# Attention and routed experts on one core: the loop body written over 24 score units, and some products issued twice

## The chip, the cores and the metric

One Trainium2 chip, one of its cores. The metric is the device time of one execution in microseconds, lower is better. Engines are called PE (TensorE), DVE (VectorE), ACT (ScalarE), POOL (GpSimd) and SP (SyncE, which here only issues transfers).

## What is computed

A block with adaptive layer norms: differential attention, then a mixture of experts with the best 2 of 8. 32 sequences (batches) of 256 tokens, 128 channels, 16 heads with two query and key vectors of 8 channels each.

```python
mod = (silu(c) @ wmod).reshape(32, 6, 1, -1)
sa, ca, ga, sb, cb, gb = ...                # ga, gb kept away from zero
h = layernorm(x) * (1 + ca) + sa
Q, K, V = h @ W_q.T, h @ W_k.T, h @ W_v.T   # per head: Q1, Q2, K1, K2 of 8 channels, V of 16
attn = softmax(mask(Q1 K1) / sqrt(8)) - lam * softmax(mask(Q2 K2) / sqrt(8))   # causal
O = rmsnorm(attn @ V) * rms_scale * 0.2
x = x + ga * (O @ W_o.T)
h = layernorm(x) * (1 + cb) + sb
logits = h @ router_w.T + router_b          # top 2 of 8, gates by softmax
x = x + gb * sum over the two chosen experts of gate * (silu(h Wg) * (h Wu)) @ Wd
```

## The kernel before, in words

The program has two stages. The first is a loop over the batches that does the attention, the second layer norm, the routing, and scatters each token's row to its two experts' places in memory. The second stage takes the rows tile by tile through the experts, and a last part adds the results. The change touches only the loop.

The loop is written out in full, one `body(i)` for each engine and iteration, with semaphores between the engines. It is a software pipeline over batches. In iteration i the engines work on the load of i+3 (`bL`: statistics of the first norm), the projections of i+2 (`bA`), the row maxima of the scores of i+1 (`b1`) and its v (`bV`), the exponentials and outputs of i (`b2`), the last outputs and the normalisation of i-1 (`bC`), the output projection and residual of i-2 (`bW`), and norm, routing and scatter of i-3 (`bR`).

The backbone is 24 **score units** for each batch. Unit n is one PSUM bank of scores: four blocks of 128x128 where n % 6 is 0 or 1, two blocks of 128x256 otherwise. `scores(bm, be, n)` issues on PE the score products of batch i+1 (into `p_max`, two banks; lines 808, 811, with the mask products at 816), and interleaved with them the transposed score products of batch i (into `p_exp`, three banks; lines 837, 840). One kind sits in the upper half of the array's rows and the other in the lower half. DVE reduces the `p_max` bank to row maxima (`take_max`, line 1190). ACT takes the exponential of the `p_exp` bank (`exp_bank`, line 1009), and POOL masks it (`mask_bank`, line 1430). The maxima of half a batch (12 units) are split in two bfloat16 parts (`minus_max`, lines 1201 and 1204), turned by PE (`max_to_rows`, line 890), copied by ACT (`copy_max`, line 1014) and moved by SP into two rows of the query operand (`move_max`, line 771), so that the product of batch i subtracts them by itself.

Everything else is placed between the units. Before the change it is written over s = 0 to 15, where an even s has one unit and an odd s has two (n = s + s//2). On PE these are: `outputs(b, g)` (line 866) for each of 8 pairs of heads, at even s; the transposes of xn (909); the two projections (`project`, 882); the transposes of on_tok (918) and the output projection (930); the transposes of h2 (944); the router's product (950); the transposes of the outputs (`outputs_to_rows`, 876); v (957); and the ranks (966). They all write the two banks of `p_mix`; the order in which each bank is used is written by hand in MISC0 and MISC1, and `mix_free` lets a step wait for the reader of the step before it. Each engine takes its instructions strictly in the order in which they are written, so a step that waits holds up the units behind it.

One chain goes through memory. `project` (PE) -> `high_part` (ACT, line 1020) -> `rest_part` (DVE, 1210) -> `middle_part` (ACT, 1024) -> `low_part` (POOL, 1436) splits q (j = 0) and k (j = 1) of batch i+2 into three bfloat16 parts. When both low parts are there (`l_ready`), SP writes the parts to memory with nine transfers (lines 726 and 730), moves the maxima (771), and when the writes have landed reads them back in the layout that the score products want (`load_unit(b, 0)`, four transfers for each of two halves, lines 756 and 761), then `mods` (746) and the next `x` (707). The loaded operands are what unit 0 of the next iteration waits for:

```python
                if n in (0, NBANKS // 2):
                    wait(pe, unit_loaded[n // (NBANKS // 2)], b)
```

The reading in SP's body, which the change leaves as it is:

```python
                b = i.plus(2)
                if active(b):
                    wait(sp, parts_saved, b)
                    load_unit(b, 0)
```

## Time and profile before

| | |
|---|---|
| median of 3 runs | 1679.91 us (1677.23 to 1682.1) |
| the profiled execution's own time | 1678.91 us |
| its span, first to last instruction | 1677.1 us |
| mean granted TensorE clock | 0.903 of full |
| PE busy / PE weight loads busy | 1340.8 us (80%) / 940.4 us (56%) |
| DVE busy | 1228.7 us (73%) |
| ACT busy | 859.4 us (51%) |
| POOL busy | 857.3 us (51%) |
| DMA, mean | 90 GB/s |

How to read it: matmuls are pipelined, and the busy time of PE holds the depth of that pipeline, so 80% is not 80% of what PE could do. The granted clock is the share of full speed (2.4 GHz) that PE was given; 0.5 is 1.2 GHz. A busy share is a mean over two stages that have different limits. In the timelines, "x4" is four instructions of one kind merged into one line with the time from the first start to the last end, and the bracket is idle time of the engine before it, with what ended it.

### The profile page before, as it was taken

Reading aid. Unit: us, or ns where it says so; the run is one execution under the profiler, and the core shown is the slowest. Engines: PE = TensorE matmul, PEld = TensorE weight load, DVE = VectorE, ACT = ScalarE, POOL = GpSimd, SP = SyncE. Lnnn points to the kernel's source line nnn. Section 1 sums busy time; section 2 is a strip of 40 time slices with the busy share of each in tenths; the row PEclk is TensorE's granted clock in tenths of the full one; section 3 lists DMA queues with packets and bytes.
Section 4 is the critical chain, followed back from the end, with each engine's and each line's share of the span. In section 5 each row is a group of like instructions: output and inputs, shape, how many; then the busy total and the mean of one; then the engine's idle time right before and its main releaser. Section 6 shows DMA issues by size and latency. Waiting matters only on the chain. (4 is left out here: it accounts for less than half of the span.)

```text
span 1677.1 us, 44178 instructions
## 1 busy us (share of the span) xinstructions
PE 1340.8 (80%) x14048; PEld 940.4 (56%) x14049; DVE 1228.7 (73%) x3090; ACT 859.4 (51%) x1918; POOL 857.3 (51%) x1283
## 2 busy tenths in 40 slices
PE   1578888888888888888888888885199999999960
PEld 0345555555555555555555555553178888888850
DVE  3467887888888888888888888876756666666647
ACT  1156667666766676667666766664123333333320
POOL 0135566666666666666666666665323333333334
PEclk9999989998999899989998999896589999999985
DMA  5453444344434443444344434410111111111129
GB/s 203 99 111 76 112 109 101 86 111 109 105 85 108 112 105 84 111 111 105 83 111 111 106 83 108 105 39 17 43 44 44 44 44 46 43 44 45 44 76 296
DMA packets 182624, 151.73 MB, mean 90 GB/s; under 512 B 29555, under 2 KB 165369, under 8 KB 182068
## 3 DMA queue, kind: packets, MB, share of 16 engines
q1 hardware_dynamic: 165124, 122.11, 30.2%
q0 software_dynamic: 8448, 16.93, 3.3%
q10 hardware_dynamic: 8880, 10.49, 1.8%
q8 instruction: 97, 1.59, 0.4%
q14 instruction: 75, 0.61, 0.1%
HBM read 88.26 MB, written 60.51 MB: 89 GB/s over the span
## 5 line engine op out<-in xcount | busy, mean ns | idle before, releaser
L1190 DVE TENSOR_REDUCE mx<-p_max 128x2 f32<-128x512 f32 (+1 forms) x768 | 504.9, 685 | 198.3 <-PE p_max L816 188.9
L1009 ACT ACTIVATE probs<-p_exp 128x512 f32<-128x512 f32 x768 | 440.4, 601 | 239.7 <-PE p_exp L837 150.9
L1430 POOL TENSOR_SCALAR_AFFINE_SELECT probs<-probs 128x256 f32<-128x256 f32 (+1 forms) x768 | 366.3, 486 | 344.6 <-ACT probs L1009 333.3
L866 PE MATMUL p_out<-probs,v 128*32 128x256 f32 (+1 forms) x4096 | 253.3, 371 | 42.1 <-ACT ot L1000 35.7
L659 POOL DMA_INDIRECT pair_out<-on,v x136 | 133.7, 983 | 282.4 <-ACT on L569 274.6
L808 PE MATMUL p_max<-kt,qt 50*128 50x256 bf16 x1024 | 199.3, 293 | 35.6 <-ACT probs L1009 19.0
L866 PEld LDWEIGHTS p_out<-probs,v 128*32 128x32 f32 x4096 | 124.0, 119 | 145.2 <-POOL probs L1430 67.9
L837 PE MATMUL p_exp<-qt,kt 52*128 52x256 bf16 x1024 | 205.2, 289 | 0.0
L816 PE MATMUL p_max<-tri,ids 64*128 64x128 bf16 (+1 forms) x768 | 188.7, 253 | 0.0
L633 DVE TENSOR_TENSOR ot<-ot,p_max 128x512 f32<-128x512 f32 x136 | 93.5, 688 | 123.6 <-PE p_max L520 105.0
L816 PE MATMUL p_max<-tri,idb 64*128 64x128 bf16 (+1 forms) x768 | 172.3, 252 | 0.0
L1477 POOL DMA_INDIRECT rows_sorted<-h,idx x128 | 128.3, 1003 | 81.2 <-DVE idx L1392 53.0
L811 PE MATMUL p_max<-kt,qt 50*128 50x128 bf16 x1024 | 115.5, 235 | 60.2 <-DMA kt<-k_parts 27.7
L569 ACT ACTIVATE on<-p_exp,v 128x128 f32<-128x128 f32 x136 | 50.0, 368 | 195.8 <-PE p_exp L551 195.8
L551 PE MATMUL p_exp<-wd,rest 128*128 x1088 | 143.9, 275 | 0.9 <-ACT on L569 0.9
L551 PEld LDWEIGHTS p_exp<-wd,rest 128*128 128x128 f32 x1088 | 132.2, 192 | 1.3 <-issue 1.3
L811 PEld LDWEIGHTS p_max<-kt,qt 50*128 50x128 bf16 x1024 | 64.7, 100 | 118.7 <-issue 66.1
L563 ACT ACTIVATE ot<-p_exp 128x512 f32<-128x512 f32 x136 | 81.5, 599 | 93.3 <-PE p_exp L520 93.3
L808 PEld LDWEIGHTS p_max<-kt,qt 50*128 50x128 bf16 x1024 | 73.1, 99 | 93.5 <-DVE mx L1190 66.8
L840 PE MATMUL p_exp<-qt,kt 52*128 52x128 bf16 x1024 | 108.9, 232 | 0.2
L1000 ACT ACTIVATE ot<-p_out,out_scale 128x256 f32<-128x256 f32 x256 | 108.0, 483 | 0.0
L1436 POOL TENSOR_TENSOR part_l<-rest,part_m 128x512 bf16<-128x512 f32 x64 | 74.1, 1158 | 64.8 <-ACT part_m L1024 64.8
(174 smaller groups left out, 2750.5 us busy)
## 6 DMA issues: line engine op xcount, KB each, us to landing
qt<-q_parts SPq DMA_DIRECT2D x128, 192.0 KB
q_parts<-part_h SPq DMA_DIRECT2D x96, 128.0 KB, 1.9
kt<-k_parts SPq DMA_DIRECT2D x128, 96.0 KB
v<-rows_sorted SPq DMA_DIRECT2D x136, 65.0 KB, 1.8
q_parts<-part_m SPq DMA_DIRECT2D x64, 128.0 KB, 1.9
kt<-k_parts SPq DMA_DIRECT2D x128, 64.0 KB
qt<-pair_out SPq DMA_DIRECT2D x32, 256.0 KB, 5.0
mods<-mod_rows SPq DMA_DIRECT2D x32, 192.0 KB
```

The lines of the kernel that those rows point to most:

```text
L551: m = nc.tensor.matmul(p_down, hid_t[:, jd.c % 2, f * P:(f + 1) * P], wd[:, bass.ds(w0 + f * P, P)], start=(f == 0), stop=(f == FCH - 1))
L659: nc.gpsimd.indirect_dma_start(pair_out, bass.IndirectOffsetOnAxis(rows_in[:, j.slot, DIM:DIM + 1].bitcast(U32), 0), rows_out[:, j.slot, : ...
L808: yield nc.tensor.matmul(p_max[:, bank, j * SEQ:(j + 1) * SEQ], qt[rows, slot, h, P:SEQ], kt[rows, slot, h, :], start=(j == 0), stop=False)
L811: yield nc.tensor.matmul(p_max[:, bank, j * P:(j + 1) * P], qt[rows, slot, h, 0:P], kt[rows, slot, h, 0:P], start=(j == 0), stop=False)
L816: m = nc.tensor.matmul(blocks[:, :, c:c + LANE], (idb if half == t else ids)[masks, :], tri4[masks, 0:len(heads), :], start=False, stop=(h ...
L837: m = nc.tensor.matmul(p_exp[:, bank, j * SEQ:(j + 1) * SEQ], kt[rows, slot, h, 0:P], qt[rows, slot, h, :], start=True, stop=True)
L840: m = nc.tensor.matmul(p_exp[:, bank, j * P:(j + 1) * P], kt[rows, slot, h, P:SEQ], qt[rows, slot, h, P:SEQ], start=True, stop=True)
L866: m = nc.tensor.matmul(p_out[32 * j:32 * j + 32, pair, SEQ - n:SEQ], v[:, b.par, tile, 2 * g + head, :], src, start=(tile == 0), stop=(til ...
L1009: nc.scalar.activation(probs[:, quad % 2, k, :], p_exp[:, n % 3, :], ACT.Exp, scale=SCALE).then_inc(exp_done.sem, 1)
L1190: V.reduce_max(mx[:, w, tile, t, heads[0]:heads[-1] + 1], p_max[:, bank, :].rearrange("p (h k) -> p h k", h=len(heads)), AX.X, negate=True ...
L1430: G.affine_select(out=blocks, in_=blocks, compare_op=ALU.is_ge, fill=zero, base=0, pattern=[[0, count], [1, P]], channel_multiplier=-1).th ...
L1477: G.indirect_dma_start(rows_sorted, bass.IndirectOffsetOnAxis(idx[:, bR.par, k:k + 1].bitcast(U32), 0), h2[:, bR.par, k // NT, k % NT, :], ...
```

## The change

The four loop bodies of PE, ACT, DVE and POOL are written over u = 0 to 23, one score unit for each u, and the other steps are given a new u each. SP's body, the units themselves and the steps' instructions stay. The order of four uses of `p_mix` changes with them. And `scores` issues the exponentials' products of six units twice, both times to the same bank; only the second issue signals ACT.

```diff
-        MISC0 = [(ht_ready, 1, 2), (r_ready, 1, 2), (r_ready, 2, 2), (on2_ready, 4, -1),
+        MISC0 = [(ht_ready, 1, 2), (r_ready, 1, 2), (r_ready, 2, 2), (on2_ready, 3, -1),
                  (v_ready, 1, 1), (on2_ready, 1, 0)]
         MISC1 = [(nmt_ready, 2, 0), (ont_ready, 1, -2), (attn_scaled, 1, -2), (h2t_ready, 1, -3),
-                 (on2_ready, 3, -1), (route, 1, -3), (nmt_ready, 1, 1), (route, ROUTE_CARRY, -3),
+                 (route, 1, -3), (on2_ready, 4, -1), (nmt_ready, 1, 1), (route, ROUTE_CARRY, -3),
                  (on2_ready, 2, 0)]
...
-            def exp_unit(b, n):
+            def exp_unit(b, n, final=True):
...
-                    if j == len(heads) - 1:
+                    if final and j == len(heads) - 1:
                         m.then_inc(exp_ps.sem, 1)
                     yield m
 
+            DOUBLED = (12, 15, 16, 21, 22, 23)
+
             def scores(bm, be, n):
 
+                if n in DOUBLED and active(bm):
+                    for _ in exp_unit(be, n, final=False):
+                        pass
                 for _ in itertools.zip_longest(max_unit(bm, n), exp_unit(be, n)):
                     pass
...
-                for s in range(NH):
-                    n = s + s // 2
-                    scores(b1, b2, n)
-                    if s % 2:
-                        scores(b1, b2, n + 1)
...
+                for u in range(NBANKS):
+                    scores(b1, b2, u)
+                    if u in (0, 2) and active(bC):
+                        outputs(bC, PAIRS - 2 + u // 2)
+                    if u in (6, 8, 12, 14, 18, 20) and active(b2):
+                        outputs(b2, 2 * (u // 6 - 1) + u % 6 // 2)
...
-                    if s in (4, 6) and active(bA):
-                        low_part(bA, (s - 4) // 2)
...
+                    if u in (8, 12) and active(bA):
+                        low_part(bA, (u - 8) // 4)
```

Where each step stands, before (by the unit after which it is issued) and after:

| engine | step | after unit, before | after unit, now |
|---|---|---|---|
| PE | outputs, pairs 6 and 7 of i-1 | 0, 3 | 0, 2 |
| PE | outputs, pairs 0 to 5 of i | 6, 9, 12, 15, 18, 21 | 6, 8, 12, 14, 18, 20 |
| PE | transposes of xn | 0 | 3 |
| PE | max_to_rows, second half of i | 2 | 1 |
| PE | project q, project k | 2, 5 | 4, 7 |
| PE | transposes of on_tok; output projection | 3; 5 | 3; 5 |
| PE | transposes of h2; router | 6; 11 | 7; 9 |
| PE | outputs_to_rows of i-1, both tiles | 8, 9 | 10, 11 |
| PE | v; max_to_rows of i+1; ranks | 12; 14; 15 | 13; 14; 16 |
| PE | outputs_to_rows of i, both tiles | 20, 21 | 17, 19 |
| ACT | xn; h2's norm | 23; 23 (iteration before) | 0; 1 |
| ACT | copy_max of i; ht | 2; 0 | 1; 3 |
| ACT | copies of outputs | 5, 11, 17, 23 | 3, 9, 15, 21 |
| ACT | ont | 3 | 4 |
| ACT | high_part; middle_part of q | 2; 5 | 5; 7 |
| ACT | high_part; middle_part of k | 5; 8 | 8; 11 |
| ACT | h2t; copy of h2; gates | 6; 9; 15 | 7; 12; 13 |
| ACT | v; copy_max of i+1; logarithm; root | 12; 14; 18; 20 | 14; 15; 19; 20 |
| DVE | minus_max of i; on_tok | 0; 0 | 0; 1 |
| DVE | statistics of i+3 | 7, 9 | 2, 3 |
| DVE | rest_part q, k; xtmp | 3, 6; 6 | 6, 9; 7 |
| DVE | normalise of i-1; of i | 9, 10; 21, 22 | 11, 13; 19, 21 |
| DVE | logits; top 8; index, choice | 12; 13; 13 | 10; 11; 14, 15 |
| DVE | minus_max of i+1; statistics of i-2 | 12; 12, 13 | 12; 15, 16 |
| DVE | sum of squares; roots; rows | 16; 16, 21; 18 | 17; 18, 22, 23; 20 |
| POOL | h2 times, h2 plus | 0, 3 | 2, 4 |
| POOL | low_part q, k | 6, 9 | 8, 12 |
| POOL | residual; sum; squares | 8; 12; 14 | 9; 14; 15 |
| POOL | four scatters | 18, 20, 21, 23 | 21, 22, 22, 23 |

On DVE the steps of an odd s stand between its two units, on the other engines behind both.

## Rows read from the trace of the kernel before

**Rows 1.** The page's 40 slices of the span, PE's busy tenths and the granted clock:

```profile
PE   1578888888888888888888888885199999999960
...
PEclk9999989998999899989998999896589999999985
```

**Rows 2.** Timeline of PE (start us, us, line, out<-in), the first and the last start of unit 0:

```profile
60.41 0.60 PE L811 MATMUL p_max<-kt,qt 50*128 50x128 bf16 x4 [16.44 <-DMA kt<-k_parts]
...
1092.04 0.21 PE L811 MATMUL p_max<-kt,qt 50*128 50x128 bf16 x1 [1.14 <-issue]
```

**Rows 3.** Windows of half an iteration (stretch, its length, busy us of each engine, PEclk, DMA):

```profile
core 0: us, PE busy (x) PEld busy (x) DVE busy (x) ACT busy (x) POOL busy (x), PEclk, DMA share, GB/s
603.72:620.99 17.27, 12.85 (x169) 7.84 (x170) 15.82 (x49) 9.50 (x24) 10.59 (x17) 0.90 0.52 143
620.99:636.69 15.70, 14.60 (x190) 9.73 (x190) 12.05 (x27) 12.95 (x30) 11.13 (x20) 1.00 0.29 62
636.69:654.40 17.71, 14.13 (x170) 8.46 (x170) 15.58 (x49) 9.65 (x24) 10.78 (x18) 0.81 0.57 140
```

**Rows 4.** Windows before and inside two low stretches of the clock:

```profile
610.14:613.55 3.41, 1.86 (x26) 1.12 (x26) 3.28 (x10) 1.89 (x5) 0.99 (x3) 1.00 0.40 91
...
613.55:616.97 3.42, 3.25 (x34) 1.96 (x35) 2.72 (x13) 1.54 (x5) 1.23 (x2) 0.50 0.65 151
...
644.27:651.10 6.83, 6.56 (x62) 3.81 (x63) 5.37 (x18) 3.85 (x9) 2.99 (x5) 0.50 0.80 165
```

**Rows 5.** Timeline of SP's queue (start us, us of issuing, line, out<-in, how many):

```profile
603.55 1.43 SPq L726 DMA_DIRECT2D q_parts<-part_h  x3
...
608.42 2.41 SPq L771 DMA_DIRECT2D qt<-nmt  x4
...
614.10 1.14 SPq L761 DMA_DIRECT2D kt<-k_parts  x3
...
636.51 1.43 SPq L726 DMA_DIRECT2D q_parts<-part_h  x3
```

**Rows 6.** Timeline of POOL around low_part(1):

```profile
601.99 0.41 POOL L1430 TENSOR_SCALAR_AFFINE_SELECT probs<-probs 128x256 f32<-128x256 f32 x1
...
602.36 1.16 POOL L1436 TENSOR_TENSOR part_l<-rest,part_m 128x512 bf16<-128x512 f32 x1
...
605.24 0.64 POOL L1430 TENSOR_SCALAR_AFFINE_SELECT probs<-probs 128x512 f32<-128x512 f32 x1 [0.81 <-ACT probs L1009]
```

**Rows 7.** Windows after the loads were issued:

```profile
618.00:618.50 0.50, 0.50 (x16) 0.26 (x8) 0.50 (x2) 0.35 (x1) 0.41 (x2) 1.00 0.86 279
618.50:619.00 0.50, 0.50 (x9) 0.42 (x4) 0.47 (x3) 0.00 (x0) 0.43 (x1) 1.00 0.35 115
```

**Rows 8.** The page's DMA issues (KB each, median us from issue to landing):

```profile
q_parts<-part_h SPq DMA_DIRECT2D x96, 128.0 KB, 1.9
```

**Rows 9.** Timeline of PE, the steps of the first half:

```profile
624.39 1.10 PE L882 MATMUL p_mix<-ht,wqk 128*128 128x256 f32 x4 [0.30 <-ACT ht L1037]
...
631.73 0.44 PE L944 MATMUL p_mix<-idf,h 128*128 128x128 f32 x2 [0.33 <-DVE xtmp L1308]
...
633.50 0.28 PE L808 MATMUL p_max<-kt,qt 50*128 50x256 bf16 x1
...
633.62 0.27 PE L808 MATMUL p_max<-kt,qt 50*128 50x256 bf16 x1
...
633.93 0.86 PE L866 MATMUL p_out<-probs,v 128*32 128x256 f32 x16
...
634.72 0.66 PE L876 MATMUL p_mix<-idf,ot 128*128 128x128 f32 x4
```

**Rows 10.** Timeline of DVE in unit 6:

```profile
631.26 0.41 DVE L1308 TENSOR_TENSOR xtmp<-p_mix,mods 128x256 f32<-128x256 f32 x1
631.59 0.68 DVE L1210 TENSOR_TENSOR rest<-p_mix,part_h 128x512 f32<-128x512 f32 x1
```

**Rows 11.** Timeline of ACT, copies of the outputs and h2's activations:

```profile
620.94 0.84 ACT L1000 ACTIVATE ot<-p_out,out_scale 128x256 f32<-128x256 f32 x2
...
622.42 0.88 ACT L1104 ACTIVATE h<-xres,neg_mr,rstd 128x128 f32<-128x128 f32 x2
```

More of the change, by code:

```diff
@@ L921, in body @@
                         m.then_inc(ont_ps.sem, 1)
-                    if s == 1 and active(bA):
+                    if u == 3 and active(bA):
+                        mix_free(pe, i, 0, 0)
+                        wait(pe, xn_ready, bA)
+                        for tile in range(NT):
+                            m = nc.tensor.transpose(p_mix[:, 0, tile * P:(tile + 1) * P], xn[:, tile, :], idf[:])
+                        m.then_inc(xt_ps.sem, 1)
+                    if u == 4 and active(bA):
                         wait(pe, ht_ready, bA)
                         project(i, bA, 0, 1)
-                    if s == 3 and active(bW):
+                    if u == 5 and active(bW):
                         mix_free(pe, i, 1, 2)
@@ L952, in body @@
                         m.then_inc(lg_ps.sem, 1)
-                    if s == 8 and active(bV):
+                    if u == 10 and active(bC):
+                        outputs_to_rows(i, bC, 1, 0, 0, 3)
+                    if u == 11 and active(bC):
+                        outputs_to_rows(i, bC, 1, 1, 1, 5)
+                    if u == 13 and active(bV):
                         mix_free(pe, i, 0, 4)
@@ L1095, in body @@
-                    if s == 15 and active(bW):
-                        if not (bW.static and bW.c < 2):
-                            wait_half(act, scattered[bW.par], bW.plus(-2))
-                        wait(act, h2t_ps, bW.plus(-2))
-                        wait(act, h2_copied, bW.plus(-2))
-                        settle(act)
-                        for tile in range(NT):
-                            c = NT * NH + NT + tile
-                            nc.scalar.activation(h2[:, bW.par, 0, tile, 0:DIM], xres[:, bass.ds(bW.n * SEQ + tile * DIM, DIM)],
-                                                 ACT.Identity, bias=neg_mr[:, NT + tile:NT + tile + 1],
-                                                 scale=rstd[:, c:c + 1]).then_inc(xn2_ready.sem, 1)
@@ L1300, in body @@
                                         ALU.mult).then_inc(on_ready.sem, 1)
-                    if s == 2 and active(bA):
+                    if u == 2 and active(bL):
+                        wait_half(dve, x_loaded[bL.par], bL)
+                        settle(dve)
+                        statistics(bL, 0, stats1)
+                    if u == 3 and active(bL):
+                        for tile in range(NT):
+                            mean_and_variance(bL, 0, stats1, tile)
+                    if u == 6 and active(bA):
                         rest_part(bA, 0)
-                    if s == 4 and active(bW):
+                    if u == 7 and active(bW):
                         wait(dve, wo_ps, bW)
@@ L1339, in body @@
-                    if s == 9:
-                        if active(bR):
-                            wait(dve, route, bR, 1)
-                            settle(dve)
-                            for tile in range(NT):
-                                V.max(top8[:, tile, :], lg[:, tile, :]).then_inc(route.sem, 1)
-                        if active(bW):
-                            for tile in range(NT):
-                                mean_and_variance(bW, 1, stats2, tile)
+                                normalise(bC, 1, 0, 0, k)
@@ new lines, in body @@
+                            if active(bR):
+                                if k == 0:
+                                    wait(dve, route, bR, 1)
+                                    settle(dve)
+                                V.max(top8[:, k, :], lg[:, k, :]).then_inc(route.sem, 1)
+                    if u == 12 and active(b1):
+                        minus_max(b1, 0, 0)
+                        minus_max(b1, 0, 1)
+                    if u == 13 and active(bC):
+                        for k in range(2):
+                            normalise(bC, 1, 1, 1, k)
@@ L1393, in body @@
-                    if s == 14:
-                        if active(b2):
-                            for k in range(2):
-                                normalise(b2, 0, 0, 0, k)
-                        inverse_roots(i, [1, 2, 3, 4])
-                    if s == 15 and active(b2):
+                        wait(dve, route, bR, 10)
+                        V.reciprocal(hrow[:, 0:NT, DIM + 1], gden[:]).then_inc(route.sem, 1)
+                        V.tensor_scalar(hrow[:, :, DIM].bitcast(I32), hrow[:, :, DIM].bitcast(I32), float(2 * SEQ), None, ALU.add)
@@ L1469, in body @@
                         G.tensor_tensor(osq[:], o[:], o[:], ALU.mult).then_inc(osq_ready.sem, 1)
-                    if s in (12, 13, 14, 15) and active(bR):
-                        k = s - 12
+                    for k in {21: (0,), 22: (1, 2), 23: (3,)}.get(u, ()):
+                        if not active(bR):
+                            continue
                         if k == 0:
```

230 lines of the change are left out of this document (108 added, 122 removed).

## The prediction, before the changed kernel was built

> **What bounds the kernel now.** I read the page's 40 slices first. TensorE (PE) is 0.8 or more busy in nearly every slice of the attention loop and all but full in the expert stage behind it; the granted clock dips again and again in the loop, and behind it only where PE has little to do [rows 1]. The change touches only the loop, so the rest of the time (from about 1,210 us to the end) is taken as it is. The first products of score unit 0 run at 60.41 us in the first iteration that has them and at 1092.04 us in the last [rows 2]: 31 iterations in 1031.6 us, 33.28 us each. All that follows is an estimate of that period.
>
> Next I cut one iteration at unit 0 and unit 12 [rows 3]. The first half (620.99 to 636.69) takes 15.70 us, at full clock; PE is busy 14.60 us of it, VectorE (DVE) only 12.05. The second half takes 17.27 or 17.71 us; there DVE is busy 15.82 or 15.58 us and PE 12.85 or 14.13. So there are two regimes: PE sets the pace in units 0 to 11, DVE in units 12 to 23. In the second half the granted clock falls: PE is busy 1.86 us of the 3.41 us before the fall and 3.25 of 3.42 after it, at half clock [rows 4]. Yet where the low stretch is twice as long (6.83 us at 0.50, [rows 4]), the half is only 17.71 - 17.27 = 0.44 us longer. DVE hides most of the loss.
>
> Third, the queue that no busy share shows. SP saves the parts of q and k of the batch two ahead to memory, then loads them back into the layout of the score products. Unit 0 of the next iteration waits for that load. In one round the saves start at 603.55, as low_part(1) ends on POOL (602.36 + 1.16 = 603.52) [rows 5, 6]. Nine saves, four moves of the maxima (608.42 to 610.83) and eight loads follow, and the last loads are issued until 615.24 [rows 5]. Then come mods and x; the DMA engines are still 0.86 busy at 618.0 to 618.5 and 0.35 in the next half microsecond [rows 7]. From an issue to its landing a save takes 1.9 us [rows 8]. So the last load lands between 615.24 + 1.9 = 617.1 and 619.0. The round trip from the end of low_part(1) to the landed load is thus 13.6 to 15.5 us. I take 15.0: eight large loads share the engines, so the end of their traffic is nearer than the landing of one transfer. Unit 0 comes at 620.99, 17.5 us after low_part(1). The slack is about 2.5 us, today.
>
> **The change, part by part.** *Low part.* low_part(1) moves from after unit 9 to after unit 12 on POOL; SP's order is untouched. Before: unit 9 starts at 633.50, the saves at 636.51, 3.0 us later [rows 9, 5]. After: unit 12 has four blocks to mask, 0.64 us instead of 0.41 [rows 6], so 3.2 us after the start of unit 12. The half from unit 0 to unit 12 takes 15.7 us now. The trip then begins at 15.7 + 3.2 = 18.9 us after unit 0 instead of 636.51 - 620.99 = 15.5, even if nothing else gets slower. With 15.0 us for the trip the period is 33.9 us or more.
>
> *Steps of the first half.* Their work on PE is the same, but what covered their waits moves. (a) The transposes of h2 wait for xtmp on DVE, 0.33 us now, with one pair's output products (0.79 us, 633.93 to 634.72 for the next pair) in between [rows 9]. After, both are in unit 7 with nothing between, and DVE still has to reduce unit 7 first, then xtmp (0.33 us to the next start, [rows 10]): 0.8 us more. (b) The first projection waits 0.30 us for ht [rows 9]. After, ACT does h2's two activations (0.88 us) and the copies of the outputs (0.84 us, [rows 11]) in units 1 and 3, ahead of ht; PE has one score unit and little more to do meanwhile: 0.6 us more. (c) outputs_to_rows in unit 10 must wait for rest_part(1) in unit 9 (0.68 us, [rows 10]), where three units lay between them: 0.5 us more. Together 1.9 us; the bounds are nothing (the engines' queues absorb them) and 3.5 us (max_to_rows in unit 1, now one step behind minus_max, added, and each wait a whole reduction longer). So unit 12 starts 17.6 us after unit 0, the trip starts at 20.8 and lands at 35.8.
>
> *Doubled products.* In units 12, 15, 16, 21, 22 and 23 each exponential's product is issued twice. One of 256 columns takes the array 0.12 us (633.50 to 633.62, [rows 9]), so 0.24 us a unit, 1.4 us an iteration. They run in the other half of the rows beside the products of the maxima, and lie in the half where DVE leads: I cost them at nothing, with 1.4 us as the bound if DVE's lead is gone.
>
> *Second half.* Spreading the DVE steps moves no work out of it (one normalise comes in at unit 13, the logits and top-8 go out). Its floor stays near 15.8 us of DVE, so it could end at 17.6 + 15.8 = 33.4. The load at 35.8 is 2.4 us later: unit 0 waits, and PE, which is in order, holds the outputs and transposes of that unit back with it.
>
> *The clock.* Today it falls after the thinnest 3.41 us of PE work, and it comes back while PE is nearly always busy [rows 4]. A PE that stands before unit 0 is a new thin place, just ahead of the half in which PE leads. If the low stretch reaches 5 us into it, PE's 5 us at full clock become up to 7.5; but ACT and DVE set part of that pace. Between 0 and 2.5 us, I take 0.8, nearer to the 0.44 us that a longer low stretch costs now.
>
> Sum: 17.6 + 3.2 + 15.0 + 0.8 = 36.6 us a period, 3.3 over 33.28. Over 31 periods that is 103 us. The first three have fewer stages and so an earlier trip: less 2 us each, 97 us. The profiled execution took 1678.91 us (span 1677.1), 1.0 us under the median of 1679.91: forecast 1678.9 + 97 = 1776 us.
>
> **Rivals.** *The clock holds.* The fall follows the thinnest stretch of PE work [rows 4]; the doubled products and the even spread fill it, and PE runs at full clock throughout. The second half then runs at DVE's pace, 15.8 us for 17.5 on average [rows 3], and with a first half as now (15.7) the period is 31.5, 1.8 less: 31 x 1.8 = 56 us, 1623 us. With half of the added waits left it is 32.4 and 1652. For it: the low stretches lie just where the doubled units are. Against it: the loads must have landed by unit 0, so the trip must start 31.5 - 15.0 = 16.5 us after unit 0, and 18.9 is the earliest that I find. It decides only if the trip takes under 12.6 us, below my 13.6. Chance 0.10. (The Trainium skill says the same of the clock in "TensorE: Matmul & The Clock Gate", Part 1: the default state is throttled, and activity releases it. By that rule alone this rival would be the likeliest, at 1623 us; the trace agrees that the clock follows PE's activity, but the rule knows nothing of the transfer.)
>
> *The transfer stays hidden, the waits stay.* The trip takes 13.6 us, or the waits of the first half are absorbed: 33.4 to 33.6 us, +0.3 a period, 1688 us; with the low stretch kept (17.6 + 17.5 = 35.1) 1735. For it: what waits ahead of a projection today waits only 0.3 us. Against it: 17.6 + 3.2 + 13.6 = 34.4 is still over 33.4. Chance 0.18, two thirds of it slower than 1684.
>
> *The change does not do what it says*: the doubled products land in the same idle time and the clock falls as before. That changes the forecast by less than 1 us a period, and is inside its range.
>
> **The numbers.** Forecast, the transfer bound: chance 0.72, its own range 1698 (33.9 us a period, no added waits) to 1832 (38.2: 3 us of added waits, 15.5 for the trip, 0.8 to 1.3 for the clock). A measurement of this kernel tells about 0.3%, 5 us, from no change. Faster 0.10; within 0.3% 0.06, from the second rival; slower 0.84. The range of 1690 to 1832 leaves the first rival and the far tail out.
>
> **What would show it.** Right: a PE wait of 2 to 3 us for the DMA of kt before unit 0 in every iteration, the first save some 21 us after unit 0, the trip still near 15 us, a period near 36.6, and a thin DVE and PE just before unit 0. The steps: waits of about 1 us before the transposes of h2 and before the first projection, 0.5 before those of outputs_to_rows in unit 10. Wrong: unit 0 released by DVE's reduction of unit 22, as now. If then the granted clock is 1.00 through the loop the first rival holds; if the first half is 15.7 us, my added waits were absorbed; if loads land in 12 us, I misread the trip.

## The result and the profile after

| | before | after |
|---|---|---|
| median of 4 runs, us | 1681.01 (1677.23 to 1684.34) | 1845.24 (1839.65 to 1849.4) |
| profiled execution, us (span) | 1678.91 (1677.1) | 1849.4 (1847.6) |
| period, first to last start of unit 0 | 33.28 | 38.51 |
| low clock per iteration, us (mean of iterations 6 to 26) | 6.3 | 11.4 |
| load landed ahead of unit 0, us (mean of the same) | 2.9 | 0.05 |

The ratio of the medians on one chip is 1.0976 [1.0937, 1.1014]: 9.8% slower. The forecast was 1776 us and the range ended at 1832. The sign and the mechanism came as forecast, the size did not. The loop's 31 periods, from 60.85 to 1254.79 us, take 1193.9 us for 1031.6 before ([rows 2]): 162 of the 170 us between the two spans.

The page's slices and the row of unit 0's products, against [rows 1]:

```profile
PE   1577787888887888888887788877619999999970
...
PEclk9988889888878898888887978899658999999995
...
L811 PE MATMUL p_max<-kt,qt 50*128 50x128 bf16 x1024 | 118.7, 246 | 104.6 <-DMA kt<-k_parts 102.2
```

PE's row, which had 8 nearly everywhere, now has many 7s; the clock's, which mostly stood at 9 with dips, stands at 8. PE waited 102.2 us in all for the DMA of kt (27.7 before; some 16.5 of each lie ahead of the first iteration). PE's longest waits in the stretch from 300 to 1100 us (engine, line and what it waited for; us in total, times, longest):

```profile
PE p_max L811 <- DMA kt<-k_parts: 45.5, 20, 3.6
PE p_mix L966 <- DVE both L1358: 43.1, 21, 2.1
...
PE p_mix L938 <- DVE xtmp L1312: 22.3, 20, 1.1
...
PE p_mix L881 <- DVE rest L1208: 8.5, 21, 0.4
...
PE p_mix L887 <- ACT ht L1061: 4.2, 9, 0.6
```

The first row is the forecast wait for the load, 2.3 us a time (0.8 to 3.6). The third, fourth and fifth are the three added waits (a), (c) and (b): 1.1 us for xtmp, 0.4 for rest_part in unit 10, up to 0.6 for ht in nine of the 21 iterations. The second was not forecast: in unit 16 the products that rank the experts wait 2.05 us for DVE's sum `both`. Before, the same wait was 23.6 us over 21 times in 300 to 1000 us, 1.1 us each.

Windows of two iterations of after, unit 0 to unit 12 and unit 12 to unit 0 (columns as in [rows 3]):

```profile
core 0: us, PE busy (x) PEld busy (x) DVE busy (x) ACT busy (x) POOL busy (x), PEclk, DMA share, GB/s
593.50:614.48 20.98, 19.46 (x191) 12.18 (x192) 11.36 (x23) 13.06 (x28) 11.05 (x19) 0.76 0.24 49
614.48:633.96 19.48, 13.40 (x184) 8.38 (x184) 16.70 (x52) 10.30 (x24) 11.35 (x18) 0.91 0.57 125
...
672.18:690.79 18.61, 15.24 (x191) 10.10 (x192) 12.19 (x27) 12.87 (x29) 12.52 (x21) 1.00 0.26 60
690.79:709.74 18.95, 13.39 (x185) 8.40 (x184) 16.54 (x52) 10.30 (x24) 11.06 (x17) 0.90 0.57 131
```

The two first halves hold the same 191 products. At full clock they keep PE busy for 15.24 us, at a mean of 0.76 for 19.46; the half grows from 18.61 to 20.98 us. Over iterations 6 to 26, the six first halves with no low clock take 18.4 us on average, the six with 6.8 us of it 19.8, the six with 10 us 21.0 and the three with 13 us 22.3. Before, the low stretches lay in the second half and the first ran at 1.00 ([rows 3]). Where the clock falls shows in windows around the two waits:

```profile
619.00:622.20 3.20, 1.10 (x18) 0.87 (x19) 3.16 (x12) 1.95 (x5) 2.86 (x5) 1.00 0.82 246
622.20:626.70 4.50, 4.50 (x52) 2.71 (x53) 3.66 (x13) 1.87 (x4) 1.22 (x3) 0.70 0.25 68
630.50:633.96 3.46, 0.04 (x1) 0.00 (x1) 2.05 (x7) 1.05 (x3) 2.65 (x4) 1.00 1.06 164
633.96:640.70 6.74, 6.74 (x67) 3.46 (x68) 4.71 (x9) 3.99 (x9) 4.42 (x7) 0.52 0.69 148
640.70:646.00 5.30, 4.99 (x56) 3.62 (x54) 2.51 (x6) 4.08 (x9) 1.87 (x4) 0.97 0.01 2
```

Ahead of the ranks PE is busy 1.10 of 3.20 us, and the clock falls behind it. Ahead of unit 0 it is busy 0.04 of 3.46 us, waiting for kt, and the 6.74 us that follow run at 0.52, which is the lower level (1.2 GHz) for nearly all of it. Then it is back. Means over iterations 6 to 26: 4.5 us low behind the first wait (units 17 to 20), and 6.7 us in the first half, behind the second wait. That one does not come every time: six first halves have none of it, behind waits for kt of 0.8 to 1.5 us, and fifteen have 6.8 to 13.2 us, behind waits of 1.2 to 3.6 us. Units 0 to 5 take 11.1 us on average, for 8.7 where the clock holds (e6, below).

The transfer, on SP's queue:

```profile
617.66 1.43 SPq L726 DMA_DIRECT2D q_parts<-part_h  x3
...
622.53 3.25 SPq L771 DMA_DIRECT2D qt<-nmt  x4
...
627.97 1.14 SPq L761 DMA_DIRECT2D kt<-k_parts  x3
...
630.47 0.33 SPq L756 DMA_DIRECT2D qt<-q_parts  x1
```

and on POOL and PE, the two ends of the round trip:

```profile
616.48 1.15 POOL L1435 TENSOR_TENSOR part_l<-rest,part_m 128x512 bf16<-128x512 f32 x1
```

```profile
633.96 0.23 PE L811 MATMUL p_max<-kt,qt 50*128 50x128 bf16 x1 [3.42 <-DMA kt<-k_parts]
```

low_part(1) ends at 617.63, 3.15 us behind unit 12 (614.48), the first save starts at 617.66, and the eight loads that unit 0 needs are issued until 629.11. Their data land 4.8 us later, and unit 0 starts at 633.96, 16.3 us after low_part(1). (The row at 630.47 already belongs to the loads for unit 12, which the queue issues until 633.53.) Means over iterations 6 to 26: 11.3 us from the end of low_part(1) until the last load for unit 0 is issued and 4.3 us from there to the landing, 15.6 us together. Before, these were 11.5 and 3.75 us, 15.25 together. So a period is 20.1 + 3.2 + 15.6 = 38.9 us, where the forecast sum had 18.4 + 3.2 + 15.0 = 36.6.

### The profile page after: what moved, and what is told of

It reads as the page before. It is cut to its first block, busy times and chain, and to the rows that moved or that the text cites. A ratio compares the mean times of both kernels' runs of the same rounds, so it can differ in the third digit from the quotient of the medians.

```text
span 1847.6 us, 45079 instructions
## 1 busy us (share of the span) xinstructions
PE 1444.4 (78%) x14482; PEld 1004.4 (54%) x14483; DVE 1231.5 (67%) x3090; ACT 881.8 (48%) x1918; POOL 862.3 (47%) x1283
## 4 chain that ended last, share of the span: by engine, by line
PE 54%; SPq 16%; DMA 9%; issue 8%; DVE 6%; POOL 4%; ACT 3%; POOLq 0%; DVEq 0%; ACTq 0%
PE p_out L871 8%; PE p_exp L551 6%; DMA kt<-k_parts 6%; PE p_exp L520 6%; PE p_max L520 5%; PE p_max L808 5%; PE p_mix L887 4%; SPq L726 4%; SPq L771 4%; PE p_max L816 4%; PE p_mix L544 3%; PE p_mix L881 3%; PE p_max L811 3%; SPq L761 2%; PE p_mix L930 2%
## 5 line engine op out<-in xcount | busy, mean ns | idle before, releaser
L1188 DVE TENSOR_REDUCE mx<-p_max 128x2 f32<-128x512 f32 (+1 forms) x768 | 526.1, 686 | 361.9 <-PE p_max L816 357.9
L1009 ACT ACTIVATE probs<-p_exp 128x512 f32<-128x512 f32 x768 | 454.3, 598 | 477.2 <-PE p_exp L837 245.5
L1429 POOL TENSOR_SCALAR_AFFINE_SELECT probs<-probs 128x256 f32<-128x256 f32 (+1 forms) x768 | 373.6, 489 | 538.6 <-ACT probs L1009 535.5
L871 PE MATMUL p_out<-probs,v 128*32 128x256 f32 (+1 forms) x4096 | 266.9, 388 | 14.4 <-POOL probs L1429 13.3
L837 PE MATMUL p_exp<-qt,kt 52*128 52x256 bf16 x1334 | 234.8, 291 | 0.2 <-ACT probs L1009 0.2
L808 PE MATMUL p_max<-kt,qt 50*128 50x256 bf16 x1024 | 219.6, 300 | 12.4 <-DVE mx L1188 12.4
L816 PE MATMUL p_max<-tri,idb 64*128 64x128 bf16 (+1 forms) x768 | 200.7, 262 | 0.0
L811 PE MATMUL p_max<-kt,qt 50*128 50x128 bf16 x1024 | 118.7, 246 | 104.6 <-DMA kt<-k_parts 102.2
L816 PE MATMUL p_max<-tri,ids 64*128 64x128 bf16 (+1 forms) x768 | 200.1, 262 | 0.0
L840 PE MATMUL p_exp<-qt,kt 52*128 52x128 bf16 x1148 | 123.7, 241 | 0.0
L881 PE MATMUL p_mix<-idf,ot 128*128 128x128 f32 x512 | 100.9, 330 | 16.0 <-DVE rest L1208 13.3
```

The costliest lines, as they stand in the source:

```text
L808: yield nc.tensor.matmul(p_max[:, bank, j * SEQ:(j + 1) * SEQ], qt[rows, slot, h, P:SEQ], kt[rows, slot, h, :], start=(j == 0), stop=False)
L811: yield nc.tensor.matmul(p_max[:, bank, j * P:(j + 1) * P], qt[rows, slot, h, 0:P], kt[rows, slot, h, 0:P], start=(j == 0), stop=False)
L816: m = nc.tensor.matmul(blocks[:, :, c:c + LANE], (idb if half == t else ids)[masks, :], tri4[masks, 0:len(heads), :], start=False, stop=(h ...
L837: m = nc.tensor.matmul(p_exp[:, bank, j * SEQ:(j + 1) * SEQ], kt[rows, slot, h, 0:P], qt[rows, slot, h, :], start=True, stop=True)
L871: m = nc.tensor.matmul(p_out[32 * j:32 * j + 32, pair, SEQ - n:SEQ], v[:, b.par, tile, 2 * g + head, :], src, start=(tile == 0), stop=(til ...
L881: m = nc.tensor.transpose(p_mix[:, bank, g * P:(g + 1) * P], ot[:, w, g, tile * P:(tile + 1) * P], idf[:])
```

## The experiments

Three causes are weighed against each other: **the transfer binds** (the period is the first half, plus the way to low_part(1), plus the round trip); **the clock** that PE's two waits drop is the bulk of the loss; **the doubled products** cost time. Each expectation numbers its theories for itself and says what a number means there: "theory 2" is not the same in all of them. Where "trip" has two numbers, the first is to the landing and the second to unit 0. Means are over iterations 6 to 26, and periods are over all 31, from the first start of unit 0 to the last, unless it is said otherwise. Each kernel was timed in 3 rounds beside the kernel before on the same chip.

**The doubled products taken out of after** (e1)

```diff
-            DOUBLED = (12, 15, 16, 21, 22, 23)
+            DOUBLED = ()
```

> The changed kernel without the second issue of the exponentials' products in six units. Theory 1 (the reload of q and k sets the period: unit 0 + first half + 3.2 + 15.6 us): the doubled products are in the second half, beside the transfer, so the period stays within 0.7 us of 38.5 and the time between 1825 and 1865 us. Theory 2 (the doubled products cost PE time on the path): 1.4 us a period less, 1800 us. Theory 3 (they hold the clock up): without them the granted clock of the loop falls clearly and the time rises over 1865 us.

1876.07 us beside 1680.68, ratio 1.119 [1.1121, 1.1259]: slower than after by 31 us. The low clock is 12.8 us an iteration for 11.4, the trip is no longer (15.1 and 15.5), the first half is 21.1 us. The period is 39.2 us for 38.5, which is 20 of the 31 us; 9 lie behind the loop. So the doubled products are no cost in the new schedule: without them the low clock is longer and the time is over 1865 us, as this expectation's theory 3 (they hold the clock up) had it. That the clock alone makes the difference is not shown apart.

**Before, with low_part(1) alone moved behind unit 12** (e2)

```diff
-                    if s in (4, 6) and active(bA):
-                        low_part(bA, (s - 4) // 2)
+                    if s in (4, 8) and active(bA):
+                        low_part(bA, (s - 4) // 4)
```

> The kernel before with one edit: low_part of k is issued on POOL after unit 12 instead of after unit 9. Theory 1 (the reload binds): unit 12 starts 15.8 us after unit 0, the trip starts 3.2 us later and takes 15.6, so the period becomes 34.6 us plus up to 1 us of lost clock, for 33.3 before: 1720 to 1755 us, with PE waiting for the transfer of kt before unit 0. Theory 2 (what is slow in the changed kernel is the waits of the steps in the first half, the reload is hidden): within 10 us of 1681.

1710.17 us beside 1680.68, ratio 1.018 [1.0145, 1.0216], 10 us under what was expected. The chain is the forecast one: first half 15.8, low_part(1) done 3.3 us behind unit 12, trip 15.25 to the landing, which comes 0.05 us before unit 0 in most iterations, a period of 34.5 us over iterations 6 to 26, where the prediction had 33.9 as the least that the late low_part(1) allows. The windows of one iteration:

```profile
603.33:618.80 15.47, 14.56 (x190) 9.72 (x190) 11.75 (x26) 12.74 (x29) 9.50 (x17) 1.00 0.28 64
618.80:638.25 19.45, 13.94 (x169) 8.45 (x170) 16.75 (x51) 11.34 (x29) 13.36 (x21) 0.82 0.51 127
```

The second half is no longer DVE's 15.8 us but what the transfer leaves. One step on one queue makes 29 us; the whole change makes 164.

**The doubled products alone, in before** (e3)

```diff
+            DOUBLED = (12, 15, 16, 21, 22, 23)
+
...
+                if n in DOUBLED and active(bm):
+                    for _ in exp_unit(be, n, final=False):
+                        pass
```

> The kernel before with the exponentials' products of units 12, 15, 16, 21, 22 and 23 issued twice, nothing else. Theory 1 (DVE and latencies set the second half, PE's extra 1.4 us lies beside them): 1675 to 1690 us. Theory 3 (the products fill the thin stretch and the clock holds): the low time of 6.3 us an iteration goes to 3 or less and the time to 1640 to 1665 us. Theory 2 (they cost PE time on the path): 1700 to 1725 us.

1690.67 us beside 1680.68, ratio 1.0058 [1.0041, 1.0074]: 10 us slower, just above the range of its theory 1. The low clock is 8.1 us an iteration, more than the 6.3 of before. One of its second halves:

```profile
606.77:624.52 17.75, 14.96 (x183) 8.91 (x181) 15.55 (x49) 9.53 (x24) 10.79 (x18) 0.81 0.59 139
```

183 products for 169 or 170 ([rows 3]; 14 more are issued, four in unit 12 and two in each of the others), and the clock at 0.81. In the old order they do not hold the clock. They are issued where PE works anyway; the waits stay. The products themselves are nearly free: a second half with 6.8 us of low clock takes 17.8 us here and 18.0 in before. But 8 of the 21 halves now have 10.2 us of low clock, and these take 19.3 us.

**After, with the chain of q and k at its old units** (e4)

```diff
-                    if u == 3 and active(bA):
+                    if u == 0 and active(bA):
...
-                    if u == 7 and active(bA):
+                    if u == 5 and active(bA):
...
-                    if u in (8, 12) and active(bA):
-                        low_part(bA, (u - 8) // 4)
+                    if u in (6, 9) and active(bA):
+                        low_part(bA, (u - 6) // 3)
```

(xn back to unit 23, and the steps of ACT and DVE between them likewise.)

> The changed kernel with the chain of q and k alone (xn, its transposes, ht, both projections, high, rest, middle and low parts) put back at the units of before, so that low_part of k follows unit 9. Theory 1 (the reload binds): its landing is hidden again, unit 0 is released by DVE, and the period is 33 to 35 us: 1670 to 1735 us. Theory 2 (the spread of the other steps makes the changed kernel slow by itself): a period of 36 us or more, over 1765 us, with unit 0 not waiting for a transfer.

1848.81 us beside 1680.68, ratio 1.0997 [1.0956, 1.1038]: no gain, where some 110 to 180 us had been expected. The transfer is hidden again, with 1.8 us of slack, and still nothing is won:

```profile
663.94:684.67 20.73, 17.86 (x190) 11.21 (x192) 12.12 (x27) 13.59 (x29) 12.93 (x21) 0.84 0.23 54
684.67:702.86 18.19, 14.56 (x184) 9.08 (x184) 15.53 (x49) 9.61 (x23) 8.82 (x16) 0.81 0.49 128
```

The time and the unhidden rest are those of the expectation's theory 2 (the spread steps are slow by themselves). The first half takes 20.9 us on average, units 0 to 5 alone 13.2 (11.1 in after), and the low clock is 13.7 us an iteration. It is not a clean reversal: steps now wait for others that moved or stayed, 1.1 us a time for ont before the output projection and 2.5 us before the ranks:

```profile
PE p_mix L966 <- DVE both L1357: 53.5, 21, 2.5
```

So the transfer alone does not explain the loss: waits inside the iteration and the clock behind them can cost as much as the transfer. That called for runs that touch the clock and nothing else.

**After, with q's saves released by low_part(0)** (e5)

```diff
-                    wait(sp, l_ready, b)
+                    wait(sp, l_ready, b, 1)
...
+                    wait(sp, l_ready, b)
```

(The second wait stands ahead of k's saves.)

> The changed kernel with one edit in SP's body: the six saves of q are issued as soon as q's low part is ready, only the three saves of k wait for k's low part. That takes 3.1 us off the trip from low_part(1) to the load (15.6 to 12.5). Theory 1 (the reload alone sets the period): 3.1 us less each, and no PE gap before unit 0, so less lost clock behind it: 35.4 us or less, 1750 us or less. Theory 4 (a second bound lies close behind: the first half is 20.1 us and the second half cannot end under some 18 us even without the transfer, as the experiment with the early chain suggests): the period only falls by 0.5 to 1.5 us, 1800 to 1830 us.

1809.18 us beside 1679.07, ratio 1.0792 [1.0754, 1.0829]: some 36 us less than after, in the range of the expectation's theory 4. The trip is 14.2 us to the landing and 14.8 to unit 0, and not 12.5: with q's saves out early, the queue stands at the moves of the maxima until ACT has written nmt. In 11 of the 21 iterations the load lands 0.3 to 2.75 us before unit 0, so the transfer no longer binds in all of them: there is a second bound close behind, and it moves with the clock (second halves with 3.4 us of low clock take 17.4 us on average, with 6.8 us 18.1, with 10.2 us 19.4). The low clock fell to 8.1 us an iteration, so both terms gained and this run doesn't part them.

**After, with 16 constant products before unit 0** (e6)

```diff
+            def filler(b, n, count):
+                ...
+                for _ in range(count):
+                    nc.tensor.matmul(p_exp[:, n % 3, 0:4 * LANE], idb[:], tri4[:].rearrange("p a k -> p (a k)"),
+                                     start=True, stop=True)
...
+                filler(b2, 0, 16)
```

They write a bank of the exponentials that the next product overwrites, and read two constants of 128 rows; nothing waits for them but PE's own order.

> The changed kernel with 16 products of constants (128 rows, 256 columns, 1.7 us at full clock) issued on PE into the free bank of unit 0 while it waits for the transfer. They do no work. Theory 3 (the first half is 20.1 us instead of 17.6 because PE comes out of its wait at half clock): units 0 to 5 take 8.5 to 9 us instead of 11.1, the low time falls from 11.4 to 5 us or less, the period to 36.4: about 1780 us. Theory 2 (the waits of the steps make the first half long): units 0 to 5 stay at 11 us, and the time within 15 us of 1845.

1789.72 us beside 1679.07, ratio 1.0643 [1.0604, 1.0682]: 56 us less than after for products that do no work. An iteration of it, against those of after above:

```profile
648.07:665.62 17.55, 15.13 (x191) 10.03 (x192) 11.21 (x25) 12.72 (x28) 11.79 (x19) 1.00 0.25 52
665.62:683.48 17.86, 15.20 (x201) 9.88 (x201) 16.30 (x51) 10.32 (x24) 10.08 (x16) 0.90 0.53 135
```

The first half has the same 191 products and is 17.7 us on average (20.1 in after), units 0 to 5 take 8.7 us (11.1). The trip is 15.3 and 15.8 us, nearly unchanged. The period is 36.6 us. This is the cleanest test of the clock term: 20.1 - 17.7 = 2.4 us, not 0.8. It may hold a little more than the clock: after's own halves with no low clock take 18.4 us and not 17.7, and in most of these the outputs of unit 2 wait some 0.9 us for POOL's masks. Measured against them, the low clock costs 20.1 - 18.4 = 1.7 us.

**The same, and 12 more before the ranks of unit 16** (e7)

```diff
+                filler(b2, 0, 16)
...
+                        filler(b2, 17, 12)
```

> As the one before, and 12 more such products (1.3 us) in unit 16, while PE waits for DVE's choice of the experts before the ranks. If the low stretch of units 17 to 20 (4.5 us at half clock) costs time of its own, the second half shortens. Theory 1 (the reload sets the end of the second half): only the low time falls, to under 3 us an iteration, and the time stays within 10 us of the kernel with the first filling alone, about 1780 us. Theory 4: 10 to 40 us less than that one.

1801.72 us beside 1679.07, ratio 1.0723 [1.0692, 1.0754]: 12 us worse than e6. Units 17 to 20 go from 6.7 to 5.2 us, but the load does not come earlier, so all of it returns before unit 0: between the last products of unit 23 and the first of unit 0 pass 3.8 us, for 2.4 in e6. The filling covers 1.9 us of that. In 13 of the 21 iterations the clock falls in the first half again (19.3 us on average), and since the first half is on the transfer's chain, that counts in full. Neither theory's range holds the result.

**Before, with 8 constant products before the ranks** (e8)

```diff
+                        filler(b2, 16, 8)
```

> The kernel before with 8 products of constants (0.86 us) before the ranks, where PE waits 1.1 us for DVE. Theory 3 (the thin stretch there lets the clock fall, and the half-clock stretch behind it costs about 1 us per 3.4 us): the low time of 6.3 us an iteration goes to under 2 and the time to 1620 to 1650 us. Theory 5 (DVE sets the second half, the clock is nearly free there, as the 0.44 us between a short and a long low stretch suggests): 1665 to 1680 us.

1629.89 us beside 1679.07, ratio 0.9704 [0.9662, 0.9747]: faster than before by 3.0%, as theory 3 had it. The clock row of its page, against [rows 1]:

```profile
PEclk9979999999999999999999999995599999999985
```

and the filling in unit 16, ahead of the ranks:

```profile
584.21 1.05 PE L901 MATMUL p_exp<-tri,idb 128*128 128x256 bf16 x8
585.40 0.17 PE L979 MATMUL p_mix<-both,beforeb 128*128 128x16 bf16 x1
```

1.05 us of products stand where PE waited 1.1 us for `both`. The low clock is 1.1 us an iteration for 6.3, the period 31.6 us, and the slack of the load 1.2 us for 2.9. One of its second halves that still have a low stretch:

```profile
578.42:595.67 17.25, 13.94 (x177) 8.71 (x178) 15.69 (x49) 9.78 (x24) 10.54 (x17) 0.90 0.58 143
```

Seven halves have 3.4 us of low clock like this one and take 17.3 us, as the three of that kind in before do, so that the two kernels compare; the fourteen with none take 16.0; the other eighteen of before, with 6.8 us, take 18.0. So the low clock of before is not nearly free: 6.8 us of it cost 2.0 us of a second half, though DVE is the busier engine there. Theory 5, and with it the prediction's "DVE hides most of the loss", falls.

The period is also that of the prediction's "clock holds" rival (31.5 us), reached from before by another and smaller edit.

**After, with both fillings and q's saves early** (e9)

```diff
+                    wait(sp, l_ready, b, 1)
...
+                filler(b2, 0, 16)
...
+                        filler(b2, 17, 12)
```

> The changed kernel with both fillings (16 products before unit 0, 12 before the ranks) and the early saves of q. Theory 1 with the clock term (what makes the changed kernel slow is the transfer, and the clock that falls behind the PE gap that it leaves, and nothing else of size): first half 17.7 us, second half ending by DVE at some 15.5 us, transfer 17.7 + 3.2 + 12.5 = 33.4: a period of 33.5 to 34 us, 1685 to 1705 us. Theory 4 (a further bound of the spread schedule at 36 to 37 us): over 1760 us.

1728.91 us beside 1682.37, ratio 1.0255 [1.0213, 1.0296]: between the two ranges, for the trip is 14.4 us, only 1.2 shorter. The low clock is 0.8 us an iteration, the load lands 0.05 us before unit 0, and the period is 17.7 + 3.2 + 14.4 = 35.3 us. So with the clock held the transfer binds. What holds SP now, over 300 to 1000 us:

```profile
SPq L772 <- ACT nmt L1029: 83.8, 39, 3.4
```

It waits 39 times there for the maxima, 2.1 us a time and two times an iteration, where in after it was once an iteration: an order of SP's own that the early saves ran into.

**e6, with the second projection ahead of the transposes of h2 in unit 7** (e10)

```diff
+                    if u == 7 and active(bA):
+                        project(i, bA, 1, 2)
...
-                    if u == 7 and active(bA):
-                        project(i, bA, 1, 2)
```

> The changed kernel with the filling before unit 0, and in unit 7 the second projection issued ahead of the transposes of h2, so that its 1.03 us lie in PE's wait of 1.1 us for xtmp. Theory 1 (the trip starts where the first half ends, so a wait of the first half is on the path): the first half is 0.9 us shorter and the period too, about 28 us off the 1790 of the filling alone: 1755 to 1770 us. Theory 6 (such waits are absorbed by DVE or ACT one unit later): within 8 us of 1790.

1762.34 us beside 1682.37, ratio 1.0467 [1.043, 1.0503]: 27 us under e6. Unit 7 takes 2.10 us for 2.97, the first half 16.9 for 17.7:

```profile
632.49:649.19 16.70, 15.36 (x192) 10.09 (x192) 11.21 (x25) 12.67 (x28) 11.79 (x19) 1.00 0.25 55
```

The projection covers the wait for xtmp, and 0.8 us of first half come back as 0.7 us of period (21 of the 27 us; the other 6 lie behind the loop). The added waits were real and lay on the transfer's chain.

**Before, with e8's filling and q's saves early** (e11)

```diff
+                    wait(sp, l_ready, b, 1)
...
+                        filler(b2, 16, 8)
```

> The kernel before with the filling before the ranks (1630 us, the load lands 1.2 us before unit 0 on average) and the early saves of q as well. Theory 1 (the load lands in time): no change, 1622 to 1636 us. If in some iterations the transfer already binds, up to 0.4 us a period comes off: 1615 to 1622 us.

1621.04 us beside 1682.37, ratio 0.9627 [0.9597, 0.9657]: the fastest of all here. The time lies between the two ranges that were given, the period says the first: it is that of e8 (31.59 and 31.60), though in e8 the load landed only 0.05 us ahead in three of 21 iterations and here in none: the slack was no limit of weight. The two profiled executions are 2.4 us apart, for which the earlier first start of unit 0 (58.1 us instead of 60.8) accounts; what makes up the rest of the 9 us between the medians is not shown (e8's own spread is 1621.73 to 1633.2). Its iteration:

```profile
560.20:575.71 15.51, 14.59 (x190) 9.72 (x190) 12.09 (x27) 12.76 (x29) 12.58 (x21) 1.00 0.40 101
575.71:591.60 15.89, 12.69 (x177) 7.96 (x178) 15.47 (x49) 9.66 (x24) 9.37 (x16) 1.00 0.53 119
```

At full clock PE's second half is 12.69 us of work, and the half is DVE's 15.5. Beside e8's row at 0.90 (17.25 us, the same 177 products), 3.4 us of low clock cost 1.36 us in this half.

**e7, with the load for unit 0 issued ahead of the saves** (e12). It reads the parts of q and k of the batch before, so the scores are those of wrong operands; the amounts moved and computed are the same.

```diff
+                if active(b) and b.c > 1:
+                    load_unit(b, 0, 1)
...
-                                 q_parts[bass.ds(b.n, 1), t, :, :, w * HU:(w + 1) * HU, :]
+                                 q_parts[bass.ds(b.n - back, 1), t, :, :, w * HU:(w + 1) * HU, :]
```

> The changed kernel with both fillings, and the load for unit 0 issued before this round's saves instead of behind them, from the rows that the batch before had saved. It reads the operands of the wrong batch, so it leaves out what the transfer has to wait for and its output is not the reference's; products, steps and bytes are the same. It shows the spread schedule without the round trip and nearly without the lost clock. Theory 1 with the clock term: 17.7 us for the first half and DVE's 15.5 for the second, a period of 33.2, about 1675 us, and PE never waits for kt. Theory 4 (a further bound of 35 us or more in the spread schedule): over 1725 us.

1704.6 us beside 1679.76, ratio 1.0153 [1.0136, 1.017]: between the two ranges again. PE never waits for kt and the low clock is gone:

```profile
596.31:613.87 17.56, 15.15 (x192) 10.05 (x192) 11.21 (x25) 12.71 (x28) 11.79 (x19) 1.00 0.23 49
613.87:630.69 16.82, 15.14 (x212) 10.28 (x212) 16.32 (x51) 10.30 (x24) 10.12 (x16) 1.00 0.59 151
```

The period is 34.0 us over all 31, and 34.4 in iterations 6 to 26. What is left is a first half of 17.6 us for 15.8 and a second of 16.8, which only the full clock brings under the 17.9 of before. Not all of that need be the order of the steps: this kernel still issues its 28 constant products and the 14 doubled ones. The 16 before unit 0 (1.9 us) follow unit 23's products, and unit 0 follows them, with no idle time of PE; in e4, where no transfer binds either, that gap is 0.8 us. So up to about 1 us of the period may be the filling's own.

**The loss in steps**, us a period: after 38.5; without the low clock behind unit 0's wait 36.6 (e6); with no wait for the transfer and no low clock 34.0 (e12); before 33.28; before with the clock nearly held 31.6 (e8). The order in itself costs at most 34.0 - 31.6 = 2.4 us at nearly equal clock (e12's fillings are in that number), the late transfer and the low clocks 4.5. These are differences between runs: the clock and the transfer feed each other, and shares taken in another order would come out otherwise.

## Why the prediction was wrong in size, and right in sign

*The bounds of before*: right in part. The load had 2.9 us of slack (I had about 2.5), and PE sets the first half. DVE sets the second only at full clock (15.9 us in e11, DVE busy 15.47); the 17.9 us of before hold some 2 us of low clock, which I had called hidden.

*The way to low_part(1), 3.2 us*: right, 3.16 measured, and e2 shows it alone at the forecast period (34.5 for a least of 33.9).

*The round trip, 15.0 us*: 15.6, where before's own was 15.25. Issuing is not what grew: it takes 11.3 us, for 11.5 before (the moves of the maxima are longer in the row above, 3.25 us for 2.41, but the queue makes that up). The landing comes 4.3 us behind the last issue, for 3.75 before and some 3.3 in my sum. In after the loads for unit 12 are issued 2.2 us before unit 0's have landed, in before 2.3 us behind them; whether that is the reason was not tried. The miss is 0.6 us a period, 19 us in all, just past the upper bound of 15.5.

*The added waits, 1.9 us*: right in sum by e6, where the first half is 17.7 us for 17.6 forecast; in after itself the halves with no low clock take 17.8 to 18.7. Of the parts, (a) came with 1.1 us of idle time for 0.33 before, 0.8 more as forecast; (c) with 0.4 for 0.5; (b) was overrated: in e6 the projection waits 0.6 us for ht, 0.3 more than before and not 0.6. Some 0.5 us of the longer half is no wait at all: PE is busy 15.13 us in e6's row for 14.60 before ([rows 3]). e10 took (a) back and won 27 us.

*The clock, 0.8 us*: this is the step that failed. It measured 2.4 us (20.1 in after, 17.7 in e6), at the upper bound of 2.5 that I had written down and set aside. I took 0.8 as "nearer to the 0.44 us that a longer low stretch costs now". But 0.44 us is what 6.8 us of low clock cost over 3.4 us of it, read from one pair of halves. It is not the price of a low stretch, and in before every second half of iterations 6 to 26 has one, so that price could not be read there. With e8 it can: 16.0 us with none, 17.3 with 3.4 us, 18.0 with 6.8 us. So a stretch as usual in before costs 2.0 us, and most of it comes with the first 3.4 us. It is also not true that the second half hides the loss and the first does not: in the first half of after 6.8 us of low clock cost 1.4 us (18.4 to 19.8) against its own halves, and 10 us cost 2.6. I also let it last 5 us; its mean is 6.7. Against the chosen value 1.6 us are missing, times 31 is 50 us. Measured against after's own halves with no low clock the term is 1.7 us; then 0.9 us of the miss are the clock's and 0.7 the first half's waits. Either way it is the largest miss of the sum, at two to three times the 0.8. (In "TensorE: Matmul & The Clock Gate", Part 1, the Trainium skill calls the throttled state the default, which activity releases. The trace agrees: 0.04 us of work in 3.46 are followed by 6.74 us at 0.52.)

*The first three iterations, less 2 us each*: against the steady 38.9 us the first periods are 32.6, 33.6 and 38.7, 12 us less and not 6. That took 6 us off the miss. Another 8 us came behind the last start of unit 0 (592.8 us to the end of the span for 585.1), which the sum took as it was.

Together, with 3 us for the 0.1 us of the added waits: 97 + 50 + 3 + 19 - 6 + 8 = 171 us, beside 170 between the profiled executions.

*The doubled products, nothing*: nearly right, for the wrong reason. They have no cost in after, where the kernel without them is 31 us slower (e1). In before they cost 10 us (e3), by a longer low clock and not by their own time, and not because DVE's lead hides them.

*The second wait*: missed. In unit 16 the ranks wait 2.05 us for DVE's `both`, where they waited 1.1. I priced the spread of DVE's steps at nothing and did not look at who waits for the last step of the choice of experts. As long as the transfer binds, its price is small: e7 fills it and wins nothing.

*The range* failed with the clock: its upper end, 38.2 us a period, held 3 us of added waits and 0.8 for the clock, though the clock term's own bound was 2.5. With that bound and the forecast's own waits (17.6 + 3.2 + 15.5 + 2.5 = 38.8) it would have reached about 1850 us.

*The rivals*: "the clock holds" did not happen here, but e8 shows that its period (31.5 us forecast, 31.6 measured) was real, and got from before by 8 products in PE's wait. "The transfer stays hidden" fell: in each of iterations 6 to 26 the load landed 0.04 to 0.06 us before unit 0.

## What to carry to other kernels

Before a step is moved, follow its result through every queue to the one that needs it, and count from there; a transfer with 2.9 us of slack in 33 has no busy share that warns of it. A wait of PE is to be priced with the clock that it drops behind it, and a low stretch is to be priced against a stretch that has none of it, not against a shorter one: the difference of the two was 0.44 to 0.7 us here where the price was 2.0. That another engine is busier there does not make it free. Where PE must wait a microsecond or two, a few constant products of all rows in front of the waiting one can be worth more than a new order of the whole loop: 8 of them made 1679 us into 1630, while the new order made 1845. They have to cover the wait: 1.9 us of them in 3.8 us did not hold the clock (e7).

## What the runs showed of the hardware that I had not expected

- A wait of about 1.1 us before the ranks was enough for the 6.3 us of low clock an iteration in before: 8 products of 128 rows and 256 columns in it (1.05 us) leave 1.1 us of it.
- More products do not by themselves mean more clock. The doubled ones (52 rows, 14 more in the second half) raised the low clock in before from 6.3 to 8.1 us; the 8 of 128 rows, placed in the wait, took it to 1.1. Whether it is the rows or the place was not tried apart.
- A low stretch costs about as much in the half where DVE is the busier engine as where PE is: 6.8 us of it make a second half of before 2.0 us longer (16.0 to 18.0), and a first half of after 1.4 us (18.4 to 19.8).
- The loss comes behind the wait, not in it: the granted clock is given as 1.00 over 630.50 to 633.96 in after, where PE did next to nothing, and as 0.52 over the next 6.74 us. The engine that waited pays when it works again.
- Issuing is the larger part of the round trip: from 617.66 to 629.11 us SP issues 21 transfers for q, k and the maxima, 11.4 of the 16.3 us, and the last of them land 4.8 us later. Taking six of the nine saves out from behind low_part(1) shortened the trip to the landing by 1.2 to 1.4 us only (e9, e5).
